# Two score units in a row, then both masks, and both exponentials in a row, at every second position

## The reference

```python
qkv = x @ w_qkv.T                                  # 16 heads of 16
q, k = rope(rms_norm(q, q_norm_w)), rope(rms_norm(k, k_norm_w))
attn = einsum('bhqd,bhkd->bhqk', q, k) * 16 ** -0.5
attn = softmax(where(causal, -inf, attn), axis=-1)
x = layernorm(x + einsum('bhqk,bhkd->bhqd', attn, v) @ w_proj.T)
normed = rms_norm(x) * norm_weight                 # eps 1e-8
shared = relu(normed @ sw1 + sb1) @ sw2 + sb2
comb = top 2 of 8 of sigmoid(normed @ router_w.T), scaled to sum 1
routed = sum over experts e of comb[:, e] * (relu(normed @ ew1[e] + eb1[e]) @ ew2[e] + eb2[e])
x = layernorm(x + shared + routed)
```

## Time and profile before

| what | value |
|---|---|
| median of 3 runs | 952.51 us (952.02 to 952.53) |
| the profiled execution, its own time | 957.52 us |
| its span, first to last instruction | 955.8 us |
| PE busy | 896.0 us (94%), 9049 instructions |
| ACT busy | 615.3 us (64%), 1060 instructions |
| DVE busy | 576.6 us (60%), 1152 instructions |
| POOL busy | 457.2 us (48%), 668 instructions |
| mean granted TensorE clock | 0.984 |

### The profile page before, as it was taken

How to read it: one execution, slowest core, us unless ns; L and a number is a source line. 1 busy time by engine, 2 the same in 40 slices (tenths; PEclk the granted TensorE clock), 3 DMA queues, 4 the chain that set the end, 5 groups by cost and what they waited for, 6 DMA issues and landing times.

```text
span 955.8 us, 26112 instructions
## 1 busy us (share of the span) xinstructions
PE 896.0 (94%) x9049; PEld 693.3 (73%) x9050; DVE 576.6 (60%) x1152; ACT 615.3 (64%) x1060; POOL 457.2 (48%) x668
## 2 busy tenths in 40 slices
PE   4789999998999989999999999999999999999995
PEld 1444555555555546888889989989899889898885
DVE  8655698889888636784344444454444433428875
ACT  4788898888878766442656655556655453667753
POOL 5344557877878636572134444344434343412211
PEclk9799999999999989999999999999999999999998
DMA  5112223433212255567882122121212121248641
GB/s 175 67 68 95 94 101 106 158 114 135 101 58 84 69 176 194 202 204 266 267 292 74 50 67 70 52 68 55 67 56 67 46 68 47 74 145 269 214 160 44
DMA packets 68706, 112.76 MB, mean 118 GB/s; under 512 B 7728, under 2 KB 46000, under 8 KB 68496
## 3 DMA queue, kind: packets, MB, share of 16 engines
q1 hardware_dynamic: 51248, 77.32, 24.5%
q10 hardware_dynamic: 10896, 16.40, 5.9%
q0 software_dynamic: 6480, 17.97, 5.2%
HBM read 66.58 MB, written 45.08 MB: 117 GB/s over the span
## 4 chain that ended last, share of the span: by engine, by line
PE 76%; ACT 7%; DVE 6%; issue 4%; POOL 2%; DMA 2%; another core or an unknown queue 1%; ACTq 1%; DVEq 0%; SPq 0%; POOLq 0%
PE hb L1811 23%; PE yb L1827 23%; PE pv_bank L1599 6%; PE slot L1577 4%; PE ma L1612 4%; PE slot L1586 3%; PE hb L1665 3%; ACT prob L872 2%; PE mb L1747 2%; PE ma L1622 1%; PE tr L1685 1%; DMA rs<-resid 1%; PE yb L1702 1%; PE mb L1735 1%
## 5 line engine op out<-in xcount | busy, mean ns | idle before, releaser
L1042 ACT ACTIVATE hf<-hb,b 128x256 f32<-128x256 f32 (+1 forms) x392 | 155.0, 454 | 206.2 <-PE hb L1811 200.7
L1811 PE MATMUL hb<-xgT,wts 128*128 128x256 f16 (+1 forms) x1872 | 213.2, 263 | 1.4 <-ACT hf L1042 1.2
L1827 PE MATMUL yb<-wts,hh 128*128 x1704 | 210.5, 273 | 0.9 <-DVE hh L1454 0.9
L1454 DVE TENSOR_TENSOR hh<-hf,hh 128x1024 f16<-128x1024 f32 (+1 forms) x98 | 120.2, 1229 | 137.3 <-ACT hh L1047 105.4
L1811 PEld LDWEIGHTS hb<-xgT,wts 128*128 x1872 | 181.2, 98 | 20.3 <-ACT hf L1042 1.0
L807 POOL DMA_INDIRECT y_tok<-yb,dest x71 | 77.8, 1096 | 227.0 <-DVE yb L1466 216.9
L1827 PEld LDWEIGHTS yb<-wts,hh 128*128 128x128 f16 x1704 | 166.3, 98 | 19.6 <-DVE hh L1454 1.2
L872 ACT ACTIVATE prob<-slot 128x1024 f32<-128x1024 f32 x160 | 161.6, 1034 | 27.8 <-PE slot L1586 27.3
L1047 ACT ACTIVATE hh<-hf 128x1024 f16<-128x1024 f32 (+1 forms) x98 | 97.6, 996 | 3.1
L741 POOL DMA_INDIRECT xg_rows<-xnh,sl_i x64 | 76.4, 1194 | 16.2 <-issue 13.9
L1577 PE MATMUL slot<-stk 64*128 64x128 f16 (+3 forms) x512 | 64.2, 308 | 16.2 <-ACT prob L872 11.6
(11 more groups left out here) (236 smaller groups left out, 1445.0 us busy)
## 6 DMA issues: line engine op xcount, KB each, us to landing
wts<-in_w_all SPq DMA_DIRECT2D x23, 512.0 KB
wts<-y_tok SPq DMA_DIRECT2D x32, 256.0 KB, 4.9
xg<-xg_rows ACTq DMA_DIRECT2D x30, 264.0 KB
stage<-in_w_all SPq DMA_DIRECT2D x12, 512.0 KB
w_split<-chunk_hl SPq DMA_DIRECT2D x12, 512.0 KB
xTf<-in_xT SPq DMA_DIRECT2D x8, 512.0 KB, 3.8
xin<-in_x SPq DMA_DIRECT2D x8, 512.0 KB
resid<-y SPq DMA_DIRECT2D x16, 256.0 KB
```

The source lines that it names most:

```text
L1042: act.activation(hf[:, c, 0:size], hb[c // 2][:, (c % 2) * TT:(c % 2) * TT + size], ACT.Relu, bias=bias, scale=1.0 / WS).then_inc(S("relu_ ...
L1454: dve.tensor_tensor(hh[:, par, 1, cs, 0:size], hf[:, cs, 0:size], hh[:, par, 0, cs, 0:size], ALU.subtract).then_inc(S("h_lo"), 1)
L1811: ins = pe.matmul(hb[hc // 2][:, (hc % 2) * TT:(hc % 2) * TT + size], weights(e, c, w, hc * P, P), xgT[:, par, x * DC + c, 0:size], start= ...
L1827: ins = pe.matmul(ybank[par][:, j * D:(j + 1) * D], hh[:, par, x, hc, P * j:P * j + P], weights(e, DC + hc * D // CH, w, hc * D % CH, D), ...
```

## The change

PE's `scores` is cut in two: `scores(b, p)` keeps the wait and the 64-row products, and `masked(p)` has the two mask products and raises `unit_ready`. `blocks(p)` holds the block lists for both. At even positions PE makes the scores of units p and p + 1 and then the masks of p and p + 1; at odd positions it makes none. ACT at even positions does the exponentials of p and p + 1 in a row, and none at odd ones. All other jobs stay at their positions. No instruction is added or removed, and no wait on a semaphore is changed in what it waits for.

```diff
                 def step(g):
                     for c, p in due(UNITS, g):
-                        exps(c, p)
+                        if p % 2 == 0:
+                            exps(c, p)
+                            exps(c, p + 1)
                     for c, i in due(AV, g - 1):
                         attended(c, i)
...
+                def blocks(p):
+
+                    g, u = p // 5, p % 5
+                    if u in (0, 2):
+                        return [(2 * g + u // 2, 0, 0)], (1, slice(0, P))
+                    if u in (1, 3):
+                        return [(2 * g + u // 2, 3, 0), (2 * g + u // 2, 1, P)], (2, slice(0, 2 * P))
+                    return [(2 * g, 2, 0), (2 * g + 1, 2, 256)], (2, slice(0, 512))
+
                 def scores(b, p):
 
-                    g, u = p // 5, p % 5
                     par = b % 2
                     i = 20 * b + p
                     if i >= 2:
                         pe.wait_ge(S("exp_done"), i - 1)
                     slot = slots[p % 2]
...
+                def masked(p):
+
+                    slot, diag = slots[p % 2], blocks(p)[1]
                     for x in range(2):
                         out = slot[:, 512 * x:512 * x + 512][:, diag[1]]
...
                         if p == 0:
                             pe.wait_ge(S("ma_free"), NTH["tq", c, NT - 1] + 1)
                             pe.wait_ge(S("mc_free"), NTH["tk", c, NT - 1] + 1)
-                        scores(c, p)
+                        if p % 2 == 0:
+                            for k in (p, p + 1):
+                                scores(c, k)
+                            for k in (p, p + 1):
+                                masked(k)
```

More of the change, by code:

```diff
@@ L1566, in scores @@
                     slot = slots[p % 2]
[L1568 to L1574, removed]
+                    for n, (pr, j, col) in enumerate(blocks(p)[0]):
                         for x in range(2):
@@ L1579, in scores @@
                                       stk[rows, par, 0, pr, P * j:T], start=(n == 0), stop=False, skip_group_check=True)
+                def masked(p):
+                    slot, diag = slots[p % 2], blocks(p)[1]
                     for x in range(2):
                         out = slot[:, 512 * x:512 * x + 512][:, diag[1]]
-                        if u == 4:
+                        if p % 5 == 4:
                             out = out.rearrange("p (i q) -> p i q", i=2)[:, :, 0:P]
```

## The result

The changed kernel takes 960.91 us (median of 4 runs, 958.14 to 962.9) where the kernel before, beside it on the same chip, takes 952.26. The ratio is 1.0096 [1.0082, 1.011]: 9 us slower, where 5.5 us faster was predicted. The profiled execution of after took 958.14 us, its span 956.4.

The account below looks back on a forecast made before the run. PE was taken as the first bound, less than 15% ahead of ACT. Batch 0 -0.5, middle batches -3.8 and batch 7 -1.2 made -5.5 us: 952.5 - 5.5 = 947.0 us, range 938 to 954.5.

Parts of the forecast that it names:

- The saving on PE: Two fewer changes between 64-row and 128-row work per pair, 0.11 us each: 0.22 a pair, 17.6 us over 80 pairs.
- the four-product units: Units loading weights twice per half, 0.33 us against 0.32: evidence that a second unit's scores follow without a price.
- A, with chunk: Batch 2, unit 0 to first `stk` copy of position 6: -0.1 us; a weight chunk at position 2, 4 or 5 adds 0.95.
- B: Batch 2, first `stk` copy of position 6 to `attended` of position 11: -1.2 us, exponential 7 being out of the way.
- C: Batch 2, `attended` of position 11 to the next unit 0: -0.15 us.
- The expected new waits: PE waits for exponentials at units 7 and 11 of 0.3 and 0.9 us, for `stk` at unit 0 about 1.0.
- Bound by its start-up: -0.5, from 0 to -1.5: Batch 0, 34.26 us busy of 42.75 and in part at half clock: -0.5 us, from 0 to -1.5.
- PE has its work done 1.0 us earlier and waits: Leg C's end, from the q/k copy of position 16 to unit 0: ACT counts there, its sum unchanged, 0.
- The clean gain: A batch without chunk or DVE limits: legs -0.1 - 1.2 - 0.15 = -1.4 us; ideal for ten pairs -2.2.
- only half stays: Batches 3 and 4 wait for DVE at L1735; gain ahead is lost, half of the rest stays: -0.7 us each.
- the slower rival: Copies behind two exponentials; q/k copy of position 4 some 1.0 us later, delaying DVE and L1735: +5, 957.5 us; chance 0.15.
- an unpaid saving: Rival: PE's saving is missing or ACT's order takes back all: 951 to 954 us; chance 0.20.

Follow-up runs that it names:

- the four units: Units 2, 3, 12 and 13 of batch 0, put back in the old order on both engines against the changed kernel: 0.39% or 3.7 us.
- apart: Changed kernel with units 2, 3, 12 and 13 of batch 0 in the old order: 957.04 us, 1.0058 of before.
- apart2: Changed kernel with units 2, 3, 12 and 13 of batch 0 in the old order, run in another group: 1.0043 of before.
- apart_filled: Changed kernel, units 2, 3, 12, 13 of batch 0 in old order, nine useless products ahead of units 0 and 10: 954.99 us, 0.9973 of before.
- apart_filled2: Changed kernel, units 2, 3, 12, 13 of batch 0 in old order plus nine useless products, run in another group: 951.07 us, 0.9991 of before.
- before_filled: Kernel before, old order on both engines, with nine useless products ahead of units 0 and 10: 956.1 us, 0.999 of before.
- the filling: Nine useless products into the idle `pv_bank` ahead of units 0 and 10, added to the changed kernel: 0.51% or 4.9 us.
- filled2: Changed kernel with nine useless products ahead of units 0 and 10, beside the unfilled one on one chip: 954.94 us, 1.0031 of before.
- again: The changed kernel once more, as it is, against before: 961.37 us, 1.0093.
- again2: The changed kernel once more, beside its filled version on one chip: 1.0082 of before; four of six runs 957.4 to 957.8 us.
- apart_filled3: Changed kernel, units 2, 3, 12, 13 of batch 0 in old order plus nine useless products, once more: 955.92 us, 0.9977 of before.
- filled: Changed kernel with nine useless products ahead of units 0 and 10: 958.41 us, 1.0017 of before.
- from1: Changed kernel with batch 0 in the old order, new order only from batch 1 on: 958.5 us, 1.0007 of before.

## Why the prediction was wrong

**The saving on PE: right.** Scores in a row, gaps before the masks halved, a pair within 0.04 us of the count, and no cost where scores follow scores, as the four-product units had said.

**Batch 2, leg by leg: near in its parts, gone in their sum.**

| leg | before | after | change | predicted |
|---|---|---|---|---|
| A, with chunk | 13.68 | 14.71 | +1.03 | +0.85 |
| B | 8.98 | 7.96 | -1.0 | -1.2 |
| C | 18.82 | 18.76 | -0.06 | -0.15 |

(The legs are measured from PE's starts: unit 0 at 125.02, L1629 at 139.73, `attended` at 147.69, unit 0 at 166.45.) Each leg misses by 0.1 to 0.2 us, all to the same side, and the batch's gain was 0.5: it measured 0.05. The expected new waits are there: 0.36 and 0.52 at units 6 and 7 (for 0.3, or 1.25 with the chunk), 0.16 and 0.52 at units 10 and 11 (for 0.9), 1.08 at unit 0 (for 1.0). ACT's idle time before the q/k copy of position 16 did not go; it fell to 1.87 us from 2.40. What is saved in B is what the chunk costs in A.

**Batch 0: the step that failed first.** "Bound by its start-up: -0.5, from 0 to -1.5" was no working at all: the batch was neither followed in the code nor in the timeline. It has its `ma` jobs at neighbouring positions, and a rule that moves units in pairs makes such jobs neighbours in the queue. The waits stood in the trace of before (1.96 and 0.64 us before the second product); each had a unit between the jobs to cover part of it. Priced as the legs were, two exponentials instead of one ahead of the freeing copy at two places, it would have come out as a loss. It measured +3.9 us to the last `attended`, and 0.4%, 3.7 us, in the time; with the four units apart the batch takes 45.0 us in apart and 46.4 in apart2 against 45.2. Nor do the other sixteen units show the 0.5 us that was forecast: at full clock throughout, the batch takes 42.9 us in apart_filled and apart_filled2 and 42.5 in before_filled.

**The clock: a term missing from the sum.** The prediction moved idle time of PE about ("PE has its work done 1.0 us earlier and waits") as if idle time were free. Longer waits in fewer places are not: behind 1.43 + 1.97 us of them the clock fell by half for 6.8 us while PE was the bound. By the filling it is worth 0.51%, 4.9 us: some 3 us in the usual execution, which is what batch 4 shows, and the rest through executions that are another 5 us slower.

**The clean gain: mis-sized.** Without both losses the kernel is at 0.9973, 0.9991 and 0.9977 of before (part of it, at most 0.2%, from the filling itself), so -0.9 to -2.6 us where the steps for batches 1 to 7 came to -5.0:

| batch | before | after | change | predicted |
|---|---|---|---|---|
| 1 | 40.28 | 40.96 | +0.7 | 0 |
| 2 | 41.48 | 41.43 | -0.05 | -0.5 |
| 3 | 42.70 | 42.82 | +0.1 | -0.7 |
| 4 | 44.60 | 46.91 | +2.3 | -0.7 |
| 5 | 42.20 | 42.13 | -0.1, part at half clock | -0.5 |
| 6 | 38.79 | 38.25 | -0.5 | -1.4 |
| 7 | 39.00 | 33.24 | -1.0 at most, without before's pause of 4.8 | -1.2 |

The common error is in how the legs were carried over: batch 2's three numbers were used for the rest with one correction each. At full clock batch 4 is +0.2 (filled2), so even there nothing was gained. The model followed only ACT's exponentials; DVE was taken as a cap at L1735 ("only half stays"), not at ACT's roots, which stand ahead of exponential 8 and wait for DVE's sums of squares: 5.8 us in after where before had 1.5 in all. DVE's sum and the roots behind it in batch 4, in before, then in after:

```profile
221.21 0.68 DVE L1149 TENSOR_REDUCE ssq<-sq 128x32 f32<-128x512 f32 x1
221.92 0.35 ACT L902 ACTIVATE ms<-ssq,eps 128x64 f32<-128x64 f32 x1 [0.45 <-DVE ssq L1149]
```

```profile
226.93 0.68 DVE L1151 TENSOR_REDUCE ssq<-sq 128x32 f32<-128x512 f32 x1
227.64 0.35 ACT L902 ACTIVATE ms<-ssq,eps 128x64 f32<-128x64 f32 x1 [2.36 <-DVE ssq L1151]
```

From unit 0 to these roots it is 18.41 us in before and 18.37 in after, and in batch 3 it is 18.33 and 18.22. In batch 4 DVE is busy without a break from 8 us ahead of the sum in both. ACT comes there 2 us earlier, since exponential 7 is out of the way as leg B had it, and stands. So what leg B was to save is gone in these two batches, and with it their 0.7 us each. The q/k copy of position 4 does start 0.7 us later in batch 4, as the slower rival said (10.49 us behind unit 0 for 9.77), but DVE's sum is no later for it (17.66 for 17.70), and at L1735 (now L1746) PE waits 3.0 us for 3.3. So the rival doesn't explain the result, though it had the right sign. What the batches would take without the roots' wait was not tried.

**The range** of 938 to 954.5 took its upper end from an unpaid saving. None of the cases held two independent losses.

## What to carry to other kernels

Where a loop body is regrouped over pairs of iterations, look at what becomes neighbours in every queue, the irregular first iteration above all: two jobs on one single buffer with nothing between them expose the whole turn-around. Change the order of producer and consumer together, and count in the price of every new wait of TensorE's also what the clock does behind it; a few useless matmuls in an idle bank are a cheap test of that. The best version found, the change without its four units in batch 0 and with the filling, is 0.2 to 0.3% ahead in the two groups of runs where before takes 957 us, and 0.1%, not clear of no change, in the one where it takes 952, which is hardly worth the code.

## What the hardware showed beyond that

- Useless work can pay: 135 matmuls more (9 at each of 15 places) made the changed kernel 0.51% faster and raised its mean granted clock from about 0.977 to 0.984. The Trainium skill (TensorE: Matmul & The Clock Gate, What's actually happening) has it that the clock follows how busy TensorE has been; the trace agrees, with waits of 1.43 and 1.97 us ahead of 6.8 us at 1.2 GHz. Such stretches come in some executions and not in others of the same kernel: again and again2 are traces of one kernel, and again (962.47 us) has three more of 3.4 us, from 83.8, 189.6 and 350.1 us on, and is at the last `attended` of batch 7 at 374.17 where again2 (957.79 us) is there at 369.44. Single traces are to be read with that: apart_filled2 and apart_filled3 are one kernel too, and their batch 0 takes 42.9 and 45.6 us.
- Products of 64 rows in the same row halves follow each other without a gap, though their weights are loaded anew: the scores of two units take 0.54 us to the mask where those of one take 0.32, so the second adds 0.22.
- The kernel before itself takes 957 us in some groups of runs and 952 in others. The traces of the first kind mostly hold a pause in batch 7, such as these waits of DVE and ACT in filled between 310 and 385 us:

```profile
DVE rcp L1192 <- remote: 5.4, 1, 5.4
ACT raw L877 <- remote: 3.6, 1, 3.6
```

The traces of the second kind don't. Its cause is open. It is why every ratio here is to runs of before on the same chip, and why the predicted 947.0 has to be held against 952.26. The ratio doesn't take it out in full, for it costs the old order more: before took 957.07 and 951.86 us in two groups of runs (5.2 apart), filled 958.41 and filled2 954.94 (3.5), apart_filled 954.99 and apart_filled2 951.07 (3.9). So ratios to a before of 957 come out some 0.15% lower for the changed order than ratios to 952. That is a part of why from1 is at 1.0007 while apart and apart2, which also have most of batch 0's loss away, are at 1.0058 and 1.0043. Another may be the clock: four of the thirteen runs of apart and apart2 are at 0.975, none of the ten of from1 is below 0.978. The rest is open.
